# Groups of 128 nodes in the order of their number of edge tiles, and half the scratch for GpSimd's gathers, in a graph network on one core

## The reference

```python
# layer 0: GCN
deg = segment_sum(1, dst); dis = where(deg > 0, rsqrt(max(deg, 1)), 0)
out = segment_sum((x @ W)[src] * (dis[src] * dis[dst])[:, None], dst)
x = layernorm(x + out)
# layer 1: three layers of typed attention, 8 heads of 32
for l in range(3):
    Q, K, V = typed_transform(x, W_Q[l] | W_K[l] | W_V[l], node_type)   # 4 node types
    kt = typed_transform(K[src], W_E[l], edge_type)                     # 3 edge types
    s = sum(Q[dst] * kt) / sqrt(32) * mu[l][edge_type]
    w = softmax of s over the edges of one dst
    x1 = layernorm(x + segment_sum(V[src] * w, dst) @ Wo[l] + bo[l])
    x = layernorm(x1 + gelu(x1 @ w1[l] + b1[l]) @ w2[l] + b2[l])
return layernorm(first_x + layernorm(x))
```

## Time and profile before

| | us |
|---|---|
| median of three timed executions | 7778.57 |
| lowest and highest | 7768.23 and 7786.26 |
| profiled execution: span from first to last instruction | 6558.3 |
| profiled execution: its own time | not recorded; only the span is known |
| stage index (constants and index_tiles) | 0 to 188.6 |
| stage GCN edges | 188.6 to 1278.9 |
| stage GCN nodes with the first projection | 1278.9 to 1513.6 |
| attention layer 1, 2, 3, edges | 1513.6 to 2655, 3237 to 4380, 4964 to 6098 |
| attention layer 1, 2, 3, nodes | 2655 to 3237, 4380 to 4964, 6098 to 6558.3 |

### The profile page before, as it was taken

How to read it: one execution, slowest core, us unless ns; L and a number is a source line. 1 busy time by engine, 2 the same in 40 slices (tenths; PEclk the granted TensorE clock), 3 DMA queues, 4 the chain that set the end, 5 groups by cost and what they waited for, 6 DMA issues and landing times. The chain is left out here.

```text
span 6558.3 us, 128194 instructions
## 1 busy us (share of the span) xinstructions
PE 5376.9 (82%) x28010; PEld 4214.7 (64%) x28011; DVE 4522.3 (69%) x11029; ACT 3285.2 (50%) x10707; POOL 4047.3 (62%) x3930
## 2 busy tenths in 40 slices
PE   4566666697888888999888888889997888888897
PEld 3344444496666666788766666668896666666786
DVE  7433333356888888666488888876656888888697
ACT  0333333454666666323466666652244666666443
POOL 0677777546777777233577777743356777777343
PEclk9999999998999999999999999999998999999998
DMA  4444444578777777112887777741168777777111
GB/s 137 123 141 141 140 138 142 154 262 256 233 237 234 234 235 234 31 32 79 275 254 239 234 235 238 236 137 32 32 209 266 236 236 233 238 239 234 38 48 42
DMA packets 574994, 1165.93 MB, mean 178 GB/s; under 512 B 86616, under 2 KB 334128, under 8 KB 574752
## 3 DMA queue, kind: packets, MB, share of 16 engines
q0 software_dynamic: 239984, 774.78, 40.4%
q1 hardware_dynamic: 321359, 377.52, 17.5%
q10 hardware_dynamic: 13536, 12.33, 0.6%
HBM read 966.73 MB, written 204.00 MB: 179 GB/s over the span
## 5 line engine op out<-in xcount | busy, mean ns | idle before, releaser
L1621 POOL DMA_INDIRECT at_kv<-kv_table,at_stage x1664 | 1656.4, 995 | 545.0 <-issue 403.5
L1637 ACT COPY sums<-ps x2499 | 949.8, 380 | 1141.6 <-PE ps L1733 1116.8
L1718 PE MATMUL ps<-at_wv,at_hot 128*128 128x264 f32 x3328 | 1026.7, 403 | 348.5 <-ACT at_hot L1654 194.4
L1621 POOL DMA_INDIRECT at_kv_last<-kv_table,at_stage_last x832 | 824.7, 991 | 273.1 <-issue 205.4
L764 POOL DMA_INDIRECT gc_rows<-x_scaled,gc_stage x832 | 807.4, 970 | 269.9 <-issue 238.3
L1718 PEld LDWEIGHTS ps<-at_wv,at_hot 128*128 128x128 f32 x3328 | 515.1, 191 | 613.7 <-DVE at_wv L1820 354.4
L1733 PE MATMUL ps<-sums,at_hot_t 128*128 x3328 | 873.7, 386 | 26.7 <-DVE at_prod L1802 20.9
L825 PE MATMUL ps<-gc_rows,gc_hot 128*128 128x256 f32 x1664 | 552.4, 428 | 287.3 <-DMA gc_rows<-x_scaled,gc_stage 286.8
L1802 DVE TENSOR_TENSOR at_prod<-ps,at_kv 128x512 f32<-128x512 f32 x832 | 571.5, 687 | 285.5 <-DMA at_kv<-kv_table,at_stage 265.3
L1701 PE MATMUL ps<-zeros_b 128*128 128x264 bf16 x2508 | 695.8, 278 | 32.5 <-PEq L93 19.0
L1733 PEld LDWEIGHTS ps<-sums,at_hot_t 128*128 128x128 f32 x3328 | 579.2, 194 | 188.5 <-issue 19.9
(11 more groups left out here) (411 smaller groups left out, 10812.2 us busy)
## 6 DMA issues: line engine op xcount, KB each, us to landing
kv_table<-pj_v_next SPq DMA_DIRECT2D x98, 396.0 KB, 3.5
kv_table<-pj_k_next SPq DMA_DIRECT2D x98, 384.0 KB, 2.8
at_hot_t<-hot_columns SPq DMA_DIRECT2D x104, 256.0 KB, 4.2
at_kv<-kv_table,at_stage POOLq DMA_INDIRECT x1664, 3.8
at_hot<-hot_rows SPq DMA_DIRECT2D x104, 256.0 KB, 4.8
at_rec<-block_records SPq DMA_DIRECT2D x104, 226.0 KB, 4.1
kv_table<-pj_v SPq DMA_DIRECT2D x49, 396.0 KB, 3.2
kv_table<-pj_k SPq DMA_DIRECT2D x49, 384.0 KB, 2.6
```

The lines of the kernel that those rows point to most:

```text
L1621: nc.gpsimd.indirect_dma_start(kv[:, 2 * k + j, :], None, g.tab_d.rearrange("t n c -> (t n) c"), bass.IndirectOffsetOnAxis(index, 0)).then ...
L1637: act.copy(dest, source).then_inc(evacuated, 1)
L1718: mm = t.matmul(own[j], hot[:, slot % HRING, j, :], wv[:, slot % WRING, j, :], start=False, stop=True, skip_group_check=True)
```

## The change

The 48 whole windows are ranked by their number of tiles, fewest first, ties by their number; window 48 and the empty one stay last. From then on "window" in all tables means the rank, and `window_rows` holds each rank's first node row. The change touches:

- `constants`: the transposition of the node types goes (one PE transpose, two small DVE operations, and the four operations for `type_hot`, which move to `index_tiles`).
- `index_tiles`: between the tile counts and the tile starts DVE computes an order value, its rank, and by one more PE step spreads four ranked rows and the node types; two more masks and 7 more PE matmuls give the degrees both by rank (`dis[:, 0]`) and by node (`dis[:, 1]`). SP stores one more block of zeros.
- `gcn_nodes`: x is loaded window by window, 49 loads of 128 KB in place of five, and before each load SP reads a word of `window_rows` into a register.
- the projections (`store_all`): before each window's wait and two stores SP reads such a word.
- the last nodes stage: each step's output store becomes two, each behind such a read.
- the kernel object is made with `dynamic_dma_scratch_size=8192` where the default is 16384.

```diff
+def window_row(nc, g, eng, at):
+    _, (row,) = nc.values_load_multi_w_load_instructions(
+        g.window_rows[0:1, bass.ds(at, 1)], [eng.engine], skip_runtime_bounds_check_because=IN_RANGE)
+    return nc.s_assert_within(row, 0, RANKED * P, skip_runtime_bounds_check_because=IN_RANGE)
@@ constants
-                t.transpose(g.ps[:, 0, 0:WINDOWS], type_rows_f[:], g.ident[0:WINDOWS, 0:WINDOWS]).then_inc(turned, 1)
-                v.tensor_copy(type_col[:], g.ps[:, 0, 0:WINDOWS]).then_inc(masks, 1)
-                for k in range(NODE_TYPES):
-                    v.tensor_scalar(g.type_hot[:, :, k], type_col[:], float(k), None, ALU.is_equal)
@@ index_tiles, sync
-                sp.dma_start(g.x_d[0:N, :], g.x).then_inc(stored, 16)
+                sp.dma_start(g.x_pad[0:N, :], g.x).then_inc(stored, 16)
+                sp.dma_start(g.x_d[FILLED * P:NPAD, :], g.zeros[:, 0:D]).then_inc(stored, 16)
@@ index_tiles, tensor
+                t.wait_ge(ranks_ready, 1)
+                t.matmul(ps[:, 0, RANKS_AT], g.ones[:], by_rank[:].rearrange("p a w -> p (a w)"), start=True, stop=True)
+                t.matmul(ps[:, 0, TYPES_AT], g.type_rows_f[:], ranked[0:WINDOWS, :], start=True, stop=True).then_inc(ranks_spread, 1)
...
+                for k, hots in enumerate((window_hot, real_window_hot)):
+                    for c in range(CHUNKS):
+                        mm = t.matmul(ps[:, 0, 128 + k * WINDOWS:128 + (k + 1) * WINDOWS], deg_rows[:, c * P:(c + 1) * P], hots[:, c, :], ...)
@@ index_tiles, vector, between TILED and the scan
+                v.tensor_copy(work[:, WINDOW], g.iota[:, 0:WINDOWS])
+                then(v.scalar_tensor_tensor(out=work[:, ORDER, 0:RANKED], in0=work[:, TILED, 0:RANKED], scalar=64.0,
+                                            in1=g.iota[:, 0:RANKED], op0=ALU.mult, op1=ALU.add))
+                then(v.tensor_tensor(diagonal[:], work[:, 0:5], g.ident[:, None, 0:WINDOWS].to_broadcast([P, 5, WINDOWS]), ALU.mult))
+                then(v.tensor_reduce(cols[:], diagonal[:], AX.X, ALU.add))
+                then(v.tensor_scalar(smaller[:], work[:, ORDER], cols[:, ORDER:ORDER + 1], None, ALU.is_lt))
+                then(v.tensor_reduce(rank_col[:], smaller[:], AX.X, ALU.add))
+                then(v.tensor_scalar(ranked[:], g.iota[:, 0:WINDOWS], rank_col[:], None, ALU.is_equal))
+                v.tensor_tensor(by_rank[:], ranked[:, None, :].to_broadcast([P, 4, WINDOWS]),
+                                cols[:, 0:4, None].to_broadcast([P, 4, WINDOWS]), ALU.mult).then_inc(ranks_ready, 1)
+                v.wait_ge(ranks_spread, 1)
+                v.tensor_copy(type_col[:], ps[:, 0, TYPES_AT])
+                then(v.tensor_copy(work[:, 0:4].rearrange("p a w -> p (a w)"), ps[:, 0, RANKS_AT]))
+                v.tensor_scalar(g.window_rows[:], work[0:1, WINDOW], float(P), None, ALU.mult)
@@ gcn_nodes, sync
-                    sp.dma_start(y[:, some[0]:some[-1] + 1], windows_in(g.x_d, some)).then_inc(x_in[k], 16)
+                    for at in some:
+                        sp.dma_start(y[:, at, :], g.x_pad[bass.ds(window_row(nc, g, sp, at), P), :]).then_inc(x_in[k], 16)
@@ store_all
+                row = window_row(self.nc, g, sp, n)
                 sp.wait_ge(self.out_k, n + 1)
-                rows = g.tab_d[:, bass.ds(P * n, P), :].rearrange("t p c -> p t c")
+                rows = g.tab_d[:, bass.ds(row, P), :].rearrange("t p c -> p t c")
@@ attention_nodes, sync
-                            sp.dma_start(two_windows(g.out, n - 5), fin[:, 1 - b]).then_inc(stored[1 - b], 16)
+                            for w in range(2):
+                                row = whole_window_row(nc, g, sp, 2 * (n - 5) + w)
+                                sp.dma_start(g.out[bass.ds(row, P), :], fin[:, 1 - b, w, :]).then_inc(stored[1 - b], 16)
@@ kernel
-    nc = _bacc.Bacc("TRN2", target_bir_lowering=False, num_devices=1)
+    nc = _bacc.Bacc("TRN2", target_bir_lowering=False, num_devices=1, dynamic_dma_scratch_size=8192)
```

More of the change, by code:

```diff
@@ L52 @@
 ROWS = WINDOWS + 2
+RANKED = N // P
+ORDER_LAST = 60000.0
+assert RANKED == FILLED - 1 == WINDOWS - 2 and (E // P + WINDOWS) * 64 + WINDOWS < ORDER_LAST
 FIRST_ROW, ZERO_ROW, UNREAD_ROW = ROWS, ROWS + 2, ROWS + 3
@@ L239, in index_tiles @@
         end_diag = sb("ix_end_diag", [P, WINDOWS])
-        work = sb("ix_work", [P, 12, WINDOWS])
-        ints = sb("ix_ints", [P, WINDOWS], I32)
+        work = sb("ix_work", [P, 16, WINDOWS])
+        ints = sb("ix_ints", [P, 2, WINDOWS], I32)
+        diagonal = sb("ix_diagonal", [P, 5, WINDOWS])
+        cols = sb("ix_cols", [P, 5])
+        smaller = sb("ix_smaller", [P, WINDOWS])
+        rank_col = sb("ix_rank_col", [P, 1])
+        ranked = sb("ix_ranked", [P, WINDOWS])
+        by_rank = sb("ix_by_rank", [P, 4, WINDOWS])
+        type_col = sb("ix_type_col", [P, WINDOWS])
+        real_window_hot = sb("ix_real_window_hot", [P, CHUNKS, WINDOWS])
         mask = sb("ix_mask", [P, CHUNKS, WINDOWS])
@@ L386, in _ @@
                 t.wait_ge(deg_rows_ready, 1)
-                for c in range(CHUNKS):
-                    mm = t.matmul(ps[:, 0, DEG_AT], deg_rows[:, c * P:(c + 1) * P], window_hot[:, c, :],
-                                  start=c == 0, stop=c == CHUNKS - 1)
+                for k, hots in enumerate((window_hot, real_window_hot)):
+                    for c in range(CHUNKS):
+                        mm = t.matmul(ps[:, 0, 128 + k * WINDOWS:128 + (k + 1) * WINDOWS], deg_rows[:, c * P:(c + 1) * P], hots[:, c, :],
+                                      start=c == 0, stop=c == CHUNKS - 1)
                 mm.then_inc(deg_ready, 1)
@@ L487, in _ @@
                 then(v.tensor_tensor(tv[:, LIVE], tv[:, PAST], base[:], ALU.subtract))
+                then(v.tensor_tensor(mask[:], window_hot[:], work[:, WINDOW, None, :].to_broadcast(shape), ALU.mult))
+                then(v.tensor_reduce(tv[:, PAST], mask[:], AX.X, ALU.add))
+                v.tensor_tensor(real_window_hot[:], g.iota[:, None, 0:WINDOWS].to_broadcast(shape),
+                                tv[:, PAST, :, None].to_broadcast(shape), ALU.is_equal)
                 v.tensor_scalar(tv[:, WIN_P], tv[:, WIN], float(P), None, ALU.mult)
@@ L493, in _ @@
                 d.then_inc(wdiag_ready, 1)
+                for k in range(NODE_TYPES):
+                    v.tensor_scalar(g.type_hot[:, :, k], type_col[:], float(k), None, ALU.is_equal)
                 for c in range(CHUNKS):
@@ L2003, in _ @@
                     pj.store_all(sp)
-                sp.wait_ge(stored[0], 16 * ((STEPS + 1) // 2))
-                sp.wait_ge(stored[1], 16 * (STEPS // 2))
+                each = 32 if last else 16
+                sp.wait_ge(stored[0], each * (STEPS // 2) + 16)
+                sp.wait_ge(stored[1], each * (STEPS // 2))
             @block.tensor
@@ L2333, in gnn_kernel @@
                 nc.sbuf_tensor("idx_x", [P, NT], I32) as g.idx_x:
+            constants(nc, g)
             index_tiles(nc, g)
```

58 lines of the change are left out of this document (30 added, 28 removed).

## The result

| | before | after |
|---|---|---|
| timed executions, median | 7776.62 us (17) | 7808.91 us (17) |
| lowest to highest | 7743.28 to 7799.5 | 7788.92 to 7839.02 |
| ratio, 95% interval | | 1.0043, 1.0030 to 1.0057 |
| profiled execution: time, span | span 6558.3 | 7797.55, 7795.8 |

The changed kernel is 0.43% slower, some 33 us. Its profiled execution has a time only 1.75 us above its span. So the 1220 us that lie between the first trace's span and the median of before are no time around the program; the kernel before had to be traced again. That second trace is the first experiment, and most of what follows is read against it.

The account below looks back on a forecast made before the run. POOL's gathers were taken to bound the edges stages, PE the nodes stages, a DVE chain the index stage. Index 5.8 + GCN nodes 35.8 = 41.6 us, so 7778.6 + 41.6 = 7820 us (+0.53%), range 7780 to 7860.

Parts of the forecast that it names:

- GCN nodes, the main term: GCN nodes stage: 49 loads with reads delay SP's weight loads, PE's step 8 starts 34 us late; stage +35.8 us.
- the read: SP's queue in GCN nodes: reading a word takes 0.53 us, with issue and address 1.09 us per window, 53.4 in all.
- The slow start: GCN nodes, PE after the pause: two groups of transposes run slower, 1.8 us.
- Index stage, +5.8: Index stage: longer DVE chain 4.8, matmuls and wider operations 2.2, less 1.2 from constants; net 5.8 us, bounds 2 and 10.
- The DVE chain: Index stage: new DVE operations and PE trip ahead of the tile starts, 4.8 us, delaying the seven gathers; constants saves 1.2.
- The seven more degree matmuls: Index stage: 7 more degree matmuls take 7 × 3.2 / 14 = 1.6 us, with DVE waiting.
- The lower bound: Index stage: growth of only 2 us if the gathers land no later, being held by other transfers.
- Edges stages, zero: Four edges stages: window order and halved scratch cost nothing; stages stay at 1090 us (GCN) and 1140 us (attention).
- No view shows what the 1220 us hold.: Whole run: timed median lies 1220 us above the profiled span, taken as unexplained and kept as it is.
- Projections and last stage, zero: Projections' reads fit in 2.1 us free per window, cost nothing; last nodes stage at most 2 us, taken as 0.
- Slower: Whole kernel: chance 0.77 that it ends slower, against same 0.15 and faster 0.08.
- signs of being wrong: After the change: a read far from 0.5 us, weight loads in another order, or an edges stage moving over 10 us.

Follow-up runs that it names:

- the first experiment: The kernel before, unchanged, run and traced again; ratio to itself 1.0003 (0.9986 to 1.002), span 7848.3 us.
- experiment 4: Changed kernel with the projection's weight loads issued ahead of the 49 loads of x in GCN nodes; ratio to before 1.0068 (1.0048 to 1.0089).
- experiment 7: Changed kernel with weight loads ahead of x, and SP issuing the index stage's x transfers only after the seven gathers landed; ratio to before 1.0024.
- experiment 11: Changed kernel with the old window order and the 49 x loads at fixed addresses, without reads; 6577.46 us beside 6557.05 of before.
- experiment 8: Kernel before with SP waiting in the index stage until the seven gathers landed before issuing x; ratio to before 0.999 (0.9972 to 1.0008).
- experiment 2: Kernel before with only the gathers' scratch changed, 8192 in place of 16384 bytes; ratio to before 1.0019 (1.0004 to 1.0033).
- experiment 3: Changed kernel with rank from the window's number alone, so the old window order; ratio to before 1.0065 (1.0046 to 1.0085).
- experiment 5: The changed kernel run again, no edit, on another chip; ratio to before 1.0078 (1.0049 to 1.0107).
- experiment 6: Changed kernel with the gathers' scratch set back to 16384 bytes; ratio to before 1.0067 (1.0042 to 1.0093).

## Why the prediction was right, and where not

The forecast was 7820 us, +41.6 and 0.53%; measured were some 33 us and 0.43%, or by stages outside the edges 38.4 us (2103.7 − 2065.3; 39.6 by the means of four traces each). The index stage grew by 16.6 and GCN nodes by 24.6 us; the other nodes stages took 2.8 us less in this pair of traces, which is within their scatter. Step by step:

- **GCN nodes, the main term, +35.8.** The mechanism is the one that the prediction gave: SP's queue holds the weights back, PE waits in front of step 8 for `pj_mu`, and the wait goes into the stage undiminished. The traces of experiments 4, 7 and 11 show it, which take the wait away in two ways; of the timed executions those of experiment 7 follow and those of experiment 4 do not. The size was 24.6. The mis-sized term is the read: taken as 0.53 us from DVE's two words, it is 0.27 us for SP's one word here, and 0.81 us in place of 1.09 a window make 39.8 in place of 53.4 us. The slow start was put at 1.8 us and is 3.0. The Trainium skill ("DMA: Bandwidth & Descriptors", Latency and other measured facts) gives such a load a floor of some 600 ns; the trace disagrees in this stage, where all 49 reads take less (262 to 509, median 270), and in the first of the later projections they lie on both sides of it (482 to 882, median 723).
- **Index stage, +5.8.** It is 16.6 (18.9 against the first trace, where DVE had the edge lists 2.2 us earlier than in the second). The DVE chain was right (3.4 against 3.6 net). The seven more degree matmuls cost 3.0 us, not 1.6. The prediction divided the row's 3.2 us by 14, but those 14 are seven matmuls of two passes each, so seven more cost the whole 3.2 again:

```profile
L407 PE MATMUL ps<-ix_window_hot,ix_deg_rows 128*128 128x50 f32 x14 | 3.2, 420 | 1.1 <-ACT ix_deg_rows L426 1.1
L407 PE MATMUL ps<-ix_real_window_hot,ix_deg_rows 128*128 128x50 f32 x14 | 3.2, 417 | 0.0
```

  The larger miss, 9.6 us, is a step that had been allowed for on the wrong side. The lower bound spoke of gathers that land no later since other transfers hold them; no term asked whether 3.4 us would put them behind such a transfer. They do: issued from 34.2 they ran ahead of the copy of `x` (39.0), issued from 37.6 they start with it (37.6), and that copy too comes 1.4 us earlier because `constants` is shorter. Experiments 7 and 8 show the transfers of `x` as the cause, and the packets which of them: beside the copy's packets of 50000 bytes the gathers' packets go through at a sixth to a third of the rate that they have beside the loads.
- **Edges stages, zero.** Their size was wrong for the executions that are timed: 1307 and 1484 us, not 1090 and 1140. So was what bounds them there: POOL's idle time before the attention gathers is 1170.5 us in the profile after and over half of it waits for ACT and DVE, where the first trace has 64.1 us for DVE. That the change adds nothing there is shown for the instructions and the scratch where there are no pauses (experiment 11), and not settled where there are: what the ratios hold beyond the rest runs from −0.06% (the first measurement: 33 − 38 us) to 0.44% (experiment 4), and in experiments 2 to 7 it is positive each time, 0.16 to 0.44% or 13 to 35 us. Experiment 2 has only the smaller scratch of the change, experiment 6 all but that, so if this is more than scatter, neither part alone accounts for it, and the prediction's zero is wrong there by that much. The order of the windows alone is inside the same uncertainty.
- **"No view shows what the 1220 us hold."** They lie inside the edges stages, with the pauses. Keeping them as they were did no harm beyond what the last point leaves open, since the change adds nothing to those stages' instructions.
- **Projections and last stage, zero.** Right: in the first projection K stores still follow each other every 3.08 us though the read takes 0.6 us there (median), and the last nodes stage takes 461.0 in place of 459.9.
- **The chances.** Slower had 0.77, and the interval lies wholly above 1.002. Two errors of 11 us with opposite signs, the read and the queued gathers, nearly cancel, and they make the sum look better than its terms. That is luck. Two of the prediction's own signs of being wrong came: a read far from 0.5 us, and edges stages far from 1090 and 1140 us, though in both kernels.

## What to carry to other kernels

A step on a queue costs what stands behind it: write down, for each load that is moved or split, who waits for the last one behind it, and put loads with a near consumer ahead of bulk ones. When a change makes a small transfer later, even by 3 us, look which bulk transfer it now falls beside, and in what packets that one moves: here 3.4 us of delay cost 13.0. And where the profiled span and the timed median differ by a sixth, trace again before believing which engine bounds a stage.

## What the hardware showed that was not expected

The same kernel takes 6557 us on one chip and 7777 to 7844 on others. Nearly all of the difference lies in the edges stages (1282 of 1290 us). In the GCN edges stage PE stands for over 2.5 us 90 times, mostly for 3 to 5, at intervals of 12.3 us in the median; DVE and ACT stand with it, POOL for a part of it. Single steps of SP's sequencer take 0.7 us, and in the place shown the waiters go on 3.4 us after the matmul is shown as ended; whether its semaphore update or its waiters are late the trace does not tell. Of the GCN edges stage's semaphore updates the trace without pauses holds 18901, the one with pauses 5353, so its "remote" waits may be such gaps in the record. The granted clock of that stage is 0.79 in place of 0.95: PE is at 1.2 GHz for 543 us of it, 123 in the first trace, and 64 of the 90 restarts after a wait of over 2.5 us fall into such a stretch. 3328 further signals on SP did not multiply the pauses (79). Whether recording, the chip or what else runs on it makes them is open: every execution here that is timed has a span on record too.
